# A two-layer decoder kernel: last block's norms and row sums reordered around its shuffle, weights prepared in waits of the last batch, first element's loads and weight splits moved

## The reference, cut to what matters

```python
x = _layernorm(x + _L0_attn_ref(x, ...))      # self attention, 16 heads, causal, window 64, relative bias
x = _layernorm(x + _L0_xattn_ref(x, ctx, ..)) # cross attention, 16 heads of 64, rope on keys, scores clipped at 11
x = _layernorm(x + _L0_ffn_ref(x, ...))       # x and ternary weight quantized; scale = max |xn| over all elements
x = _layernorm(x + _L1_attn_ref(x, ...))      # state = tanh(state A' + u B') + sp, 256 steps in sequence
x = _layernorm(x + _L1_xattn_ref(x, ctx, ..)) # linear attention, norms on q, k, v and on the dense output
x = _layernorm(x + _L1_ffn_ref(x, ...))       # fp8 fake quantization, scale = max |x| over everything
```

## Time and profile before

| | |
|---|---|
| median of three runs | 1025.55 us |
| the profiled execution | 1023.58 us, its span 1021.9 us (1.68 us lie around the span) |
| PE busy | 910.6 us, 89% |
| DVE busy | 685.5 us, 67% |
| ACT busy | 509.7 us, 50% |
| POOL busy | 510.2 us, 50% |
| chain that ended last | PE 51%, DVE 26%, POOL 11%, ACT 6%, issue 4%, DMA 1% |

### The profile page before, as it was taken

One profiled execution on the slowest core, in us unless ns is written; L12 is line 12 of the kernel. 1 busy time (PEld: TensorE's weight loads), 2 busy tenths in 40 slices (PEclk: granted clock), 3 DMA queues, 4 the chain that ended last, 5 costly groups with the idle time before them and its releaser, 6 DMA issues.

```text
span 1021.9 us, 22090 instructions
## 1 busy us (share of the span) xinstructions
PE 910.6 (89%) x8504; PEld 646.2 (63%) x8504; DVE 685.5 (67%) x1906; ACT 509.7 (50%) x1441; POOL 510.2 (50%) x642
## 2 busy tenths in 40 slices
PE   6689999999999999999999999998988599999822
PEld 4456666666666666666666666665655389888721
DVE  6457578567767875885678578668788454444477
ACT  6656636653764566366546645663332133333324
POOL 2544475367456644654674466456756112333363
PEclk9999999999999999999999999999989599999955
DMA  7000000000000000000000000000000002212211
GB/s 198 21 6 12 1 2 6 12 1 7 12 1 1 7 11 2 6 2 12 1 6 11 2 1 1 1 2 1 22 0 1 0 12 33 31 29 33 31 13 42
DMA packets 60470, 15.09 MB, mean 15 GB/s; under 512 B 41278, under 2 KB 59726, under 8 KB 60238
## 3 DMA queue, kind: packets, MB, share of 16 engines
q1 hardware_dynamic: 60366, 13.69, 6.3%
HBM read 10.51 MB, written 3.17 MB: 13 GB/s over the span
## 4 chain that ended last, share of the span: by engine, by line
PE 51%; DVE 26%; POOL 11%; ACT 6%; issue 4%; DMA 1%; SPq 0%; POOLq 0%; DVEq 0%; ACTq 0%
PE score_banks L2132 7%; DVE o_rec L1372 7%; PE out_bank L2056 6%; DVE prob L1470 6%; PE bank_a L1752 4%; PE score_banks L2070 4%; PE score_banks L1757 4%; PE score_banks L1788 3%; PE score_banks L2260 3%; POOL psum L733 3%; POOL psum L734 2%; PE bank_d L2273 2%; PE bank_d L1773 2%; PE score_banks L1758 2%; PE score_banks L1759 2%
## 5 line engine op out<-in xcount | busy, mean ns | idle before, releaser
L1006 ACT ACTIVATE prob<-score_banks 128x1024 f32<-128x1024 f32 x128 | 131.1, 1024 | 162.0 <-PE score_banks L2132 161.6
L733 POOL TENSOR_TENSOR psum<-psum,prob 128x512 f32<-128x512 f32 x64 | 81.8, 1278 | 142.1 <-DVE prob L1470 142.1
L2132 PE MATMUL score_banks<-qh,kr 64*128 64x256 f32 x1024 | 146.2, 404 | 2.2 <-ACT qh L915 1.3
L731 POOL TENSOR_TENSOR psum<-prob 128x512 f32<-128x512 f32 x64 | 82.6, 1291 | 92.7 <-DVE prob L1470 92.6
L1372 DVE RECIPROCAL o_rec<-out_bank 128x256 f32<-128x256 f32 x64 | 111.9, 1748 | 24.3 <-PE out_bank L2064 24.3
L2056 PE MATMUL out_bank<-prob,v 128*64 128x256 f32 x1024 | 124.6, 385 | 1.4 <-DVE on L1373 1.4
L2132 PEld LDWEIGHTS score_banks<-qh,kr 64*128 64x128 f32 x1024 | 89.1, 187 | 39.7 <-issue 30.0
L866 ACT ACTIVATE prob<-prob,neg_max 128x128 f32<-128x128 f32 (+1 forms) x256 | 107.2, 427 | 5.1 <-DVE neg_max L1257 5.1
L1470 DVE TENSOR_SCALAR prob<-prob 128x1024 f32<-128x1024 f32 x128 | 101.3, 791 | 12.5 <-ACT prob L1006 12.5
L2056 PEld LDWEIGHTS out_bank<-prob,v 128*64 128x64 f32 x1024 | 67.8, 136 | 46.6 <-issue 17.2
L1055 ACT ACTIVATE prob<-score_banks 128x8 f32<-128x8 f32 x255 | 45.3, 178 | 96.2 <-PE score_banks L2260 96.2
(11 more groups left out here) (414 smaller groups left out, 2126.3 us busy)
## 6 DMA issues: line engine op xcount, KB each, us to landing
cb<-in_ctx_dram SPq DMA_DIRECT2D x8, 256.0 KB, 2.8
bias_mask<-bias_scratch SPq DMA_DIRECT2D x4, 384.0 KB, 5.4
xb<-in_x_dram SPq DMA_DIRECT2D x8, 128.0 KB, 2.1
prob<-in_L_xattn_Wkv_dram SPq DMA_DIRECT2D x1, 1024.0 KB, 8.1
x_scratch<-v SPq DMA_DIRECT2D x16, 64.0 KB, 1.5
bias_mask<-x_scratch SPq DMA_DIRECT2D x16, 64.0 KB
att_scratch<-on SPq DMA_DIRECT2D x16, 64.0 KB, 1.5
prob<-att_scratch SPq DMA_DIRECT2D x16, 64.0 KB, 3.0
```

The costliest lines, as they stand in the source:

```text
L733: link(g.tensor_tensor(psum[:, p % 2, :], psum[:, p % 2, :], pp[:, 2, :], ALU.add))
L1006: s.activation(prob[:, p % 2, 2 * u:2 * u + 2, :].rearrange("p k (h q) -> p h k q", h=2), sc[:, 0:2, :].rearrange("p h (k q) -> p h k q", ...
L2132: last = mm(sc[:, h, k * T:(k + 1) * T], kr[rows_of, p % 2, kb * P:(kb + 1) * P], qh[rows_of, p % 2, :], start=True, stop=True, skip_group ...
```

## The change

In the first element the order of loads is changed, two loads are issued by ACT, the bias round trip through DRAM goes first, `split_high` goes from ACT to DVE, two of four `split_low` go from POOL to DVE, a memset goes from DVE to POOL, the rope tables are loaded and turned later, and the first jobs use six banks. In the last batch the second bank is always `o0`, the output products are spread over the pairs, the last row sum is done by DVE, and two weight blocks of pair 7 come after it. In the joint x3's second turn has its own bank. In the recurrence late work and z products get other steps. In the tail the order of DVE, POOL, ACT, PE and SP is changed. Unlisted: declarations, and edits that only rename a bank.

```diff
+FIRST_BANKS = ("p", "d2", "s0", "s1", "o", "p", "s0")
-                add((b, p, kind), kind, target, SECOND_BANK[p])
+                add((b, p, kind), kind, target, SECOND_BANK[p] if b < B - 1 else "o0")
-LATE_Z = 29
+FIRST_LATE = 9
+Z_EARLY = (13, 14, 15, 22, 30, 38, 42, 43, 44, 45, 46, 54)
+Z_STEPS = [*Z_EARLY, *(t for t in range(64, T) if t % WINDOW_STEPS in (10, 12, 13, 14))][:3 * Z_PARTS]
@@ sync: rel, x, [qkv, proj now on ACT], ctx, then
+            sp.wait_ge(d_free, 1)
+            sp.dma_start(scratch, rel_row).then_inc(scratch_out, 16)
...             (b_proj, wk, wv, two columns, bias_mask x4, then keep, Wkv, Wq, cos, sin)
@@ sync, windows
+                    if k == WINDOWS:
+                        rows_of_x4(k)
                     sp.wait_ge(att_out, 16 * (w + 1))
...
-                if k - 1 < WINDOWS:
-                    sp.wait_ge(x4_out, 16 * k)
-                    sp.dma_start(x4_rows[...]).then_inc(x4_rows_in, 16)
+                if k < WINDOWS:
+                    rows_of_x4(k)
@@ gpsimd
+            pool.wait_ge(d_full, 2)
+            pool.wait_ge(scratch_out, 16)
+            g.memset(prob1[:, :, 0:WINDOW], 0.0).then_inc(zeros_ready, 1)
-            split_low(2, wq_s[:, 1, :], wq_nat, wq_s[:, 0, :])
-            split_low(3, wv_s[:, 1, :], wkv_nat[:, INNER:2 * INNER], wv_s[:, 0, :]).then_inc(weights_split, 1)
+                    if pair == B * PAIRS - 1:
+                        first.then_inc(last_sum_begun, 1)
+                        break
+            scale_dense(13)
             affine_of(0)
-            scale_dense(13)
-            affine_of(1)
             finish_dense(13)
             scale_dense(14)
+            affine_of(1)
             finish_dense(14)
+            scale_dense(15)
             affine_of(2)
-            scale_dense(15)
...
+            pool.wait_ge(red_ready, 3)
             for k in range(4):
                 add_bias(k)
@@ scalar
+            act.dma_start(w_nat[:, 0:3, :], a["L0_attn_w_qkv"]...).then_inc(qkv_in, 16)
+            act.dma_start(w_nat[:, 3, :], a["L0_attn_w_proj"]).then_inc(qkv_in, 16)
...             (exps_of(0, 0, 0, 1) directly after apply_norm(0); no split_high)
-            copies(WINDOWS + 1, 6)
+            for i in (6, 12):
+                copies(WINDOWS + 1, i)
             normalize_x5(0)
-            copies(WINDOWS + 1, 12)
+            copies(WINDOWS + 2, 12)
             normalize_x5(1)
-            copies(WINDOWS + 2, 12)
@@ vector, first element (new order)
+            w.tensor_copy(ctx_t[:, :], bank_p[:, :]).then_inc(ctx_kept, 1)
             for at in range(6): first_score(at)
             odd_turn(1); first_score(6); first_score(7)
+            centre_weights(); odd_turn(3); measure_kv(0, 0); split_high(0); split_high(1)
+            odd_turn(5); prepare_trig(); self_attention(0, S_CN_LOW, 0); split_high(2)
+            odd_turn(7); keep_cos(); measure_kv(0, 1); split_high(3); split_low(2)
+            odd_turn(9); invert_sums(0); odd_turn(11); self_attention(0, S_DIVIDE, 0)
+            split_low(3)
@@ vector, last batch
-                if p >= 3:
+                if 3 <= p < B - 1:
                     find_f_peak(p - 3)
+                    def add_last_sums():
+                        dve.wait_ge(last_sum_begun, 1)
+                        dve.wait_ge(clamped, 2 * pair + 2)
+                        link(w.tensor_tensor(psum.., psum.., prob[.., 2, :], ALU.add))
+                        w.tensor_tensor(psum.., psum.., prob[.., 3, :], ALU.add).then_inc(last_sum_ready, 1)
             measure(tiles_of(y, QT), 0, y_var_ready)
+            keep_last_weights()
...
             measure_f(B - 1)
+            find_f_peak(B - 3)
             normalize_f(B - 1)
+            quantize_weights()
@@ vector, windows
+                if k == WINDOWS:
+                    measure_dense(k - 4)
                 dve.wait_ge(x4_rstd, k)
                 normalize_window(W_X4, x4[:, k - 1, :], bank_d[:, 0:D]).then_inc(x4_ready, 1)
@@ vector, tail (new order)
             rectify_queries(end)
+            measure_dense(13)
             add_rows(0)
             divide_attended(end)
             normalize_dense(13)
             add_rows(1)
             measure_dense(14)
+            add_rows(2)
             normalize_dense(14)
...
+            find_peak(0)
             measure_dense(end)
+            add_rows(3, count=3)
...             (last norm chain; find_peak(1) and find_peak(2) in its waits)
+            normalize(tiles_of(x5[:, 12:15, :], 3), ...)   # now ahead of the peak of the last row
@@ tensor, end of first element
+            prep_values(JOB["values 0", 0], 0, 0)
+            self_attention(0, S_KV_SUM)
+            prep_values(JOB["values 1", 0], 0, 1)
...             (turn of lat)
+            prep_keys(JOB["keys a", 1], 0, "a")
+            prep_keys(JOB["keys b", 1], 0, "b")
             pe.wait_ge(lat_split, 1)
             prep_queries(JOB["queries", 0], 0)
@@ tensor, last batch and joint
+                if p >= 2:
+                    output_of_last(p - 2)
             values_of(B * PAIRS - 1)
+            sum_of(B * PAIRS - 1)
+            output_of_last(PAIRS - 2)
+            turn_f(B - 2)
+            output_of_last(PAIRS - 1).then_inc(y_full, 1)
+            turn_x3(0)      # bank_a
+            turn_x3(1)      # out_bank
             begin_z(0)
             begin_z(1).then_inc(c_ready, 1)
@@ tensor, steps
                 if not worked:
-                    keep_clock(KEEP_Z if busy else KEEP, spare)
-                elif not busy and i not in (0, 6):
+                    keep_clock(KEEP_Z if worked_late else KEEP, spare)
+                elif i not in (0, 6) and t > WINDOW_STEPS:
                     keep_clock(KEEP_Z, spare)
-            for k, order in ((WINDOWS, (0, 1, 2, 3, 4, 5, 8, 7, 9, 6, 11, 15)), (WINDOWS + 1, (2, 3, 4, 5, 8, 6, 11)),
+            for k, order in ((WINDOWS, (1, 6, 2, 3, 4, 5, 7, 8, 9, 11, 15)), (WINDOWS + 1, (6, 2, 3, 4, 5, 11, 8)),
```

More of the change, by code:

```diff
@@ L140, in last_o0_job @@
     return [j.done for key, j in JOB.items() if len(key) == 3 and key[0] == b and key[1] < 3 and j.bank == "o0"][-1]
+LAST_D2_JOB = [j.done for j in JOB.values() if j.bank == "d2"][-1]
 SELF_NORMS = 3
@@ L752, in _ @@
             rstd_of_f(B - 1)
-            for k in range(4):
+            for k in range(3):
                 rstd_of(NORMS, k, 4, EPS_LN, half=k % 2)
@@ L1342, in _ @@
             first_score(7)
+            centre_weights()
             odd_turn(3)
+            measure_kv(0, 0)
+            split_high(0)
+            split_high(1)
+            odd_turn(5)
+            prepare_trig()
+            self_attention(0, S_CN_LOW, 0)
+            split_high(2)
+            odd_turn(7)
+            keep_cos()
             measure_kv(0, 1)
-            odd_turn(5)
-            self_attention(0, S_CN_LOW, 0)
-            odd_turn(7)
+            split_high(3)
+            split_low(2)
             odd_turn(9)
@@ L1667, in _ @@
             measure_window(W_X4, x4_rows[:, end, :], x5_var)
-            add_rows(3, count=3)
+            find_peak(1)
             dve.wait_ge(x5_rstd, 1)
@@ L2003, in _ @@
             first_weigh(1)
+            first_turn(3)
+            first_weigh(2)
+            pe.wait_ge(kv_centred, 1)
+            pe.wait_ge(cn_kept, 1)
+            products_of_ctx(0, bank_p)
+            for at in range(4, 7):
+                first_turn(at)
+                first_weigh(at - 1)
+            pe.wait_ge(trig_ready, 1)
+            pe.wait_ge(d_free, SETUP_D + D_SCORE + 7)
+            for t, bank in enumerate((bank_d, bank_d2)):
+                for k in range(KB):
+                    last = turn(bank[:, k * P:(k + 1) * P], trig_rep[:, t, k].rearrange("p r d -> p (r d)"))
+                last.then_inc(trig_full, 1)
+            first_turn(7)
+            first_weigh(6)
             pe.wait_ge(kv_free, 1)
             products_of_ctx(1, bank_p)
-            for at in range(3, TURNS):
+            for at in range(8, TURNS):
                 first_turn(at)
@@ L2081, in turn_f, with output_of_last @@
                 last.then_inc(f_t_full, 1)
-            def beside_last_batch(p):
+            def output_of_last(p):
+                pe.wait_ge(on_ready, n(B - 1, PAIRS, p + 1))
+                for qt in range(QT):
+                    product = mm(y_last[:, qt * D:(qt + 1) * D], on[:, p, qt * P:(qt + 1) * P], wo[:, p, :],
+                                 start=(p == 0 and qt == 0), stop=(p == PAIRS - 1), skip_group_check=True)
+                return product
+            def beside_last_batch(p):
+                if p == 2:
+                    engine, count = LAST_D2_JOB
+                    pe.wait_ge(p_free[engine], count)
+                if p >= 2:
+                    output_of_last(p - 2)
                 if p == 1:
```

277 lines of the change are left out of this document (138 added, 139 removed).

## The result

Eight runs of the two kernels beside each other gave a median of 1024.64 us before (4 runs) and 1002.16 us after (4 runs, 1001.24 to 1003.16): ratio 0.978, 95% interval 0.9764 to 0.9795. The forecast was 1009.5, with 1001.5 to 1017 as its range, so the result lies 0.7 us inside the lower end. The profiled execution took 1002.82 us (span 1001.1); before it was 1023.58 (span 1021.9). So 20.8 us of span went, where the sum said 15.3.

The account below looks back on a forecast made before the run. No one engine was taken as the bound; each edge stage was read by itself. Terms 3.0 + 1.8 + 3.3 + 1.5 + 0.6 + 5.1 = 15.3 us off 1023.58 gave 1008.3, 1010.2 by the median; forecast 1009.5, range 1001.5 to 1017.

Parts of the forecast that it names:

- rival 1: First element: DVE's new work meets little of POOL's, so it gains 8 us instead of 3; 1004.5 us, chance 0.17.
- First element: 3.0: First batch element: y 1.1 us earlier plus 1.9 behind it, DVE's added work eating the earlier start; bounds -1.5 and +8.
- Rivals 1 (8 us) and 2 (-1.5): The second: first element gets longer, -1.5 instead of 3, and the tail's additions cost 2.3; 1014.6 us, chance 0.15.
- Last batch: 1.8: Last batch: gain 2.8 from the second bank less 1.0 for output products meeting PE on the chain.
- gain 2.8: Last batch, pair 3: with o0 as second bank PE is ahead again and DVE's 2.79 idle goes; bounds 0 and 3.5.
- Last row sum and quantization: 2.8: Division of the last pair 3.3 us earlier; weight quantization, moved into DVE's wait in the joint, sticks out by 0.5.
- Joint: 2.0 for the turns: Joint: x3's second turn no longer waits for the first copy and input product, gain 2.0; joint sum 1.5 us.
- Recurrence: 0.6: Recurrence: 2.8 from waits and moved late products less 1.3 at the low clock, taken as 0.6; bounds -1 and +2.
- If it comes back as long after the start as before: Recurrence: if TensorE's clock rises as late as before, 6.5 us hold 6.7 steps instead of 9, costing 1.3.
- if the clock at the first steps rose earlier: Recurrence: a sign named beforehand, clock rising earlier or later at the first steps, that would show the forecast wrong.
- Rival 4: Recurrence starts and stays at the low clock, steps of 0.97 instead of 0.57 us; up to 1032 us, chance 0.06.
- Tail: 6.8 - 1.7: Tail: 1.5 + 2.5 + 2.8 from reordering and unhindered scalings, less 1.7 for additions behind the maximum; 5.1 us, bounds 2.5 and 7.5.

Follow-up runs that it names:

- kernel 1: Changed kernel with x3's turns in the old order, the second into bank_a behind the first's copy and begin_z(0); 1006.77 us.
- experiment 9: Changed kernel with the weight splits where they were before, high parts on ACT and low parts on POOL; 1004.29 us.
- kernel 11: Changed kernel with split_high(3) and split_low later on DVE, o ahead of split_low(2), ACT's keep_kv(0, 1) behind even_turn(10), bias additions released by x5's last rows; 1001.20 us.
- Experiment 5: Kernel before the change with only o0 as second bank for every job of the last batch; 1021.85 us against 1023.77, ratio 0.9974.
- experiment 6: Changed kernel with all output products of the last batch behind its last row sum instead of spread over the pairs; 1003.02 us.
- experiments 4: Changed kernel with the last pair's last two row-sum additions on POOL again instead of DVE; 1004.10 us.
- Experiments 1 and 2: The second: changed kernel with x3's turns in the old order and 96 instead of 192 columns of keep_clock below step 9; 1008.15 us.
- Kernels 4 and 12: The second: the changed kernel, unchanged, run once more; 1001.39 us.
- experiment 3: Changed kernel without POOL's wait for the maximum ahead of the four bias additions; 1003.51 us.
- experiment 10: Changed kernel with the four bias additions released by x5's last normalized rows instead of by the maximum; 1002.28 us.
- kernels 8: Changed kernel with split_high(3) and split_low(2) behind odd_turn(11) on DVE, and ACT's keep_kv(0, 1) behind even_turn(10); 1001.10 us.

## Why the prediction was right, and where it was wrong

The direction, and each part as a gain, held. But 1002.2 us lies below the forecast's own band of 1005 to 1014, nearer to rival 1's 1004.5, whose mechanism was false; it is inside the wide range only by 0.7 us. Two stages were put too small, the batches up to `f_peak` by 2.0 and the recurrence by 2.7, together 4.7 of the 5.5 us by which the sum fell short. (The bounds of the stages add up to 0 and 26.8, not to -1 and +29; the forecast doesn't hang on it.)

**First element: 3.0, came 2.34.** The number is close because two misses cancel, which is luck. y was to come 1.1 us earlier and came 0.17 later; behind y the gain was put at 1.9 and was 2.5 (lat to first unit 3.7 us instead of 6.2). The first exponential came at 14.91, not 13.3, so 3.3 of the 4.9 us were there to be eaten. DVE did carry 18.84 of 20 us, and steps lengthened beside POOL are there: `cn_s` 2.85 beside a POOL split of 2.54, the cast behind it 1.76 against 0.66 for its like. What the term doesn't have is TensorE's clock ahead of o. It is 0.50 from 39.2 to 46.0 us, where the kernel before has 1.00, and the same element at 1.00 there (kernel 1) is 1.8 us shorter up to y. In experiment 9, with the load on ACT and POOL again, y came no earlier either (46.14), also at the low clock. The order of DVE's list holds a part: kernel 11 has y 2.3 us earlier than kernel 1, and behind y PE's list and clock take it back. How the 3.3 us divide between these is not shown. Rivals 1 (8 us) and 2 (-1.5) were false.

**Last batch: 1.8, came 3.2 at the last exponential.** The step that failed is "gain 2.8" for the bank: it counted DVE's one gap of 2.79, and the low clock in that pair, which the earlier trace rows show (0.64 at 743 to 746), was given no price. Experiment 5 has 4.14 for the whole pair by its profile, above my bound of 3.5: 1.53 us of PE's waits gone, and a unit of 1.13 us where it had 2.08, values products of 0.28 where they had 0.41. (The medians of that experiment alone would leave 2.8 open.) The output products cost 1.03 by the profile, as put (experiment 6).

**Last row sum and quantization: 2.8, came 3.4** up to `f_peak`. DVE's sums are 1.45 of it, output products out of the way 1.37 (experiments 4, 6); the weight blocks moved behind pair 7 were not tested alone. The division itself moved by 3.3, as put.

**Joint: 2.0 for the turns, came 2.4**, and 2.24 in experiment 1. What the term didn't see is what it does to the next one.

**Recurrence: 0.6, came 3.3.** The failed step is "If it comes back as long after the start as before": I carried the clock's rise over from a profile in which PE worked in pieces ahead of step 1. With turns and input products back to back it came up before the first step. The sign "if the clock at the first steps rose earlier" was named as one of being wrong, and came. Experiments 1 and 2 price it: 1.82 for this, 1.07 for fillings that I had counted as a loss of 1.3 (at a slow start). Kernels 4 and 12 show that the rise can still come behind the first tanh. Rival 4, a clock that stays down, is excluded by the steps of 0.565 us from the first on.

**Tail: 6.8 - 1.7, came 7.55 - 1.45.** Up to the issue of the last shuffle's first DMA it gained 1.6 us (put at 1.5), from there to the last measure 2.4 (2.5), and from the measure to the maximum 3.5, of which the three scalings are 2.9 (2.8). The first two are readings of the timelines, no experiment takes them apart. The lock-out by whole instructions predicted both sides of the rest: experiment 3 moves the three scalings back to 3.48 and the stretched quantizing steps back to 0.43 and 0.69. The Trainium skill, "SBUF — State Buffer", section "Who interferes with whom", says this of a VectorE copy or scaling in two-port mode, or an operation with two SBUF inputs, against a reading GpSimd operation; the trace agrees, with 3.48 against 0.85 us, and so it does where the same section says that a reduction doesn't contend on trn2: 0.28 and 0.54 beside the additions in experiment 10, as without them.

## What to carry to other kernels

Ahead of a latency-bound loop look at how TensorE arrives: putting its turns and input products back to back gained 1.8 us inside the loop beside the 2.2 of the wait. A chain that several engines feed in written order gives a gain back at the first instruction that stands ahead of the next link; when a start is moved by 3 us, follow every engine's list to the next join, not only the busiest one, and TensorE's clock with it: before an order is called the cause, compare with a profile of the unchanged code at the same clock. Count a wait's price over the whole period of the pattern, not by its longest gap.

## What was not expected of the hardware

- The same first element, instruction for instruction, had TensorE at the low clock between 38 and 48 us for 6.8 us in five of its eight profiles, for 3.4 in two and not at all in one (kernel 1). From the second kv measure to the first exponential it took 20.28 to 20.45, 19.68 to 19.74 and 18.49 us. Why the clock differs there is not known.
- At the low clock, steps with 96 columns of filling are shorter (0.67 against 0.85 us) but the slow steps lasted 10.8 instead of 5.8 us; the fuller filling won by 1.07 us.
- In the first 16 us the window rows of after give a granted clock of 1.00, as those of kernels 8 and 9 do, while eight score products take 1.44 us in after and 0.82 in the other two. The durations tell the level there, the column does not.
- Scalings of one column were not lengthened beside POOL's additions (0.15 and 0.14 us at 977.5), a product of two SBUF columns was: 0.43 us in after and 0.80 in kernel 10, against 0.16 before and in kernel 3, where no addition runs beside it.
- Five of the nine runs of the changed kernel lie at 1001.2 to 1001.5 and four at 1002.8 to 1003.8. That this is TensorE's start in the first element fits the profiles' spread there, but wasn't tested.
